# Linear attention: outputs ten chunks behind, and the image maps' small products moved behind transposes and grams

## The reference, cut to what matters

```python
qkv = x @ w_qkv.T                      # x: layer norm of h, (4, 3136, 192)
q, k, v = (qkv[0], qkv[1], qkv[2])     # 12 heads of 16 features
q = _l1_normalize(q)                   # divided by the sum over all tokens of |q|
k = _l1_normalize(k)
kv = jnp.einsum('bhnd,bhne->bhde', k, v)
out = jnp.einsum('bhnd,bhde->bhne', q, kv)
return out.transpose(0, 2, 1, 3).reshape(B, N, C) @ w_proj.T + b_proj
```

## Time and profile before

| | |
|---|---|
| median of 3 runs | 2784.31 us (2782.99 to 2789.03) |
| profiled execution | 2790.76 us, span 2788.9 us |
| mean granted TensorE clock | 0.894 |
| TensorE busy, whole span | 2293.3 us (82%) |
| VectorE busy | 2000.3 us (72%) |
| ScalarE busy | 1550.6 us (56%) |
| GpSimd busy | 996.8 us (36%) |
| the attention stage, 1883.00 to 2335.75 us | 452.75 us, TensorE clock 0.81 |

### The profile page before, as it was taken

One profiled execution on the slowest core, in us unless ns is written; L12 is line 12 of the kernel. 1 busy time (PEld: TensorE's weight loads), 2 busy tenths in 40 slices (PEclk: granted clock), 3 DMA queues, 4 the chain that ended last, 5 costly groups with the idle time before them and its releaser, 6 DMA issues. The chain is left out here.

```text
span 2788.9 us, 45419 instructions
## 1 busy us (share of the span) xinstructions
PE 2293.3 (82%) x14046; PEld 1665.0 (60%) x14047; DVE 2000.3 (72%) x5437; ACT 1550.6 (56%) x2693; POOL 996.8 (36%) x1024
## 2 busy tenths in 40 slices
PE   8999999999996888989865999926678885666665
PEld 4444444444444878888854999925576774444443
DVE  5777777777764888888853444447788877889986
ACT  2444444444444777777743566536665650777776
POOL 1100100100000355555561444468776730444443
PEclk9999999999997999999976999966787887677867
DMA  2000000000002011111125777731111100000000
GB/s 56 0 18 12 0 18 13 0 9 1 0 1 89 21 47 47 47 50 46 51 79 190 256 256 256 256 101 50 47 48 42 49 13 22 21 21 26 26 25 26
DMA packets 69143, 162.81 MB, mean 58 GB/s; under 512 B 12977, under 2 KB 32342, under 8 KB 68702
## 3 DMA queue, kind: packets, MB, share of 16 engines
q1 hardware_dynamic: 39426, 94.27, 10.3%
q0 software_dynamic: 21504, 44.99, 5.6%
q10 hardware_dynamic: 8064, 21.68, 2.6%
HBM read 63.98 MB, written 63.88 MB: 46 GB/s over the span
## 5 line engine op out<-in xcount | busy, mean ns | idle before, releaser
L211 ACT ACTIVATE prob<-pscore 128x896 f32<-128x896 f32 x336 | 308.1, 917 | 424.1 <-PE pscore L293 424.1
L418 DVE TENSOR_REDUCE pmax<-ppre 112x1 f32<-112x512 f32 x656 | 424.4, 686 | 162.7 <-PE ppre L260 162.6
L307 PE MATMUL pout<-prob,xkey 128*64 128x448 f32 x1344 | 328.3, 567 | 0.4 <-ACT prob L211 0.4
L260 PE MATMUL ppre<-xh,yh 49*112 49x512 f32 x656 | 291.5, 446 | 7.8 <-DVE pmax L418 4.1
L723 POOL DMA_INDIRECT rows_in<-xr,idx x224 | 231.4, 1033 | 154.4 <-DVE idx L1237 97.3
L1694 POOL DMA_INDIRECT yg<-rows_out,place x224 | 234.2, 1045 | 62.4 <-issue 62.1
L193 POOL CAST yh<-ynext 113x448 fp32r<-113x448 f32 x28 | 17.2, 616 | 668.1 <-DVE pmax L418 639.9
L260 PEld LDWEIGHTS ppre<-xh,yh 49*112 49x112 f32 x656 | 112.8, 172 | 239.8 <-issue 103.5
L293 PE MATMUL pscore<-yh,xh 49*128 49x448 f32 x700 | 241.3, 422 | 0.4 <-DVE yh L438 0.4
L2209 POOL TENSOR_TENSOR yg<-y,gout 112x512 f32<-112x512 f32 x112 | 141.3, 1273 | 259.1 <-DVE y L2442 259.1
L1544 POOL TENSOR_TENSOR zl<-z,zh 128x448 fp32r<-128x448 f32 x126 | 144.8, 1149 | 219.8 <-ACT zh L1510 210.3
(11 more groups left out here) (388 smaller groups left out, 6558.2 us busy)
## 6 DMA issues: line engine op xcount, KB each, us to landing
wd<-down SPq DMA_DIRECT2D x63, 512.0 KB, 3.0
xb<-rows_in SPq DMA_DIRECT2D x63, 448.0 KB, 3.6
rows_out<-yb ACTq DMA_DIRECT2D x63, 336.0 KB, 3.2
out<-ho SPq DMA_DIRECT2D x28, 336.0 KB, 2.8
rows_in<-zero SPq DMA_DIRECT2D x15, 448.0 KB
rows_in<-xr,idx POOLq DMA_INDIRECT x224
yg<-rows_out,place POOLq DMA_INDIRECT x224
xkey<-in_xkey SPq DMA_DIRECT2D x4, 800.0 KB, 6.7
```

The source lines that it names most:

```text
L211: nc.scalar.activation(prob[j % 3][:, :, :], pscore[j % 2][:, :, 0:CH], ACT.Exp).then_inc(exped, 1)
L260: pe.matmul(out[:, :], yh1[rows, q * T:(q + 1) * T], xh[b % 2][rows, block * 512:(block + 1) * 512], start=True, stop=True, tile_position= ...
L307: mm = pe.matmul(pout[i * LO:(i + 1) * LO, 0:CH], xkey[b % 2][:, 2 * j + i, :], prob[j % 3][:, i, :], start=(j == 0), stop=(i == 1 and j = ...
L418: nc.vector.reduce_max(pmax[:, q, 2 * block + half:2 * block + half + 1], bank(u, depth), AX.X).then_inc(pre_max, 1)
```

## The change

The lag of the outputs goes from nine chunks to ten and the ring from ten to eleven. On TensorE a step always begins with transposes and gram; the small products come behind them, and where there are outputs, the keys map, the projection and the image map come behind these. On VectorE `low` always opens a step; `values_mapped` moves behind `add_experts` of its step, `keys_mapped` and `map_projected` behind `add_moe`, and `image_mapped` behind `add_out`. Behind the loop one more chunk of outputs is left, and stands between values map and projection.

```diff
-    LATE = CPI + 2
+    LATE = CPI + 3
     RING = LATE + 1
...
             for s in range(NC):
                 b, c = divmod(s, CPI)
+                transposes(s)
+                gram(s, b, c)
+                if b and c == 0:
+                    turn_gram(b - 1)
                 if b and c == 1:
                     values_map(b - 1)
+                if s >= LATE:
+                    map_out(s - LATE)
                 if b and c == 2:
                     image_map(b - 1)
-                transposes(s)
-                if b and c == 0:
-                    turn_gram(b - 1)
-                gram(s, b, c)
                 if b and c == 0:
                     keys_map(b - 1)
                 if b and c == 1:
                     project_map(b - 1)
-                if s >= LATE:
-                    map_out(s - LATE)
...
             map_out(NC - LATE + 1)
             values_map(B - 1)
+            map_out(NC - LATE + 2)
             project_map(B - 1)
             image_map(B - 1)
-            for n in range(NC - LATE + 2, NC):
+            for n in range(NC - LATE + 3, NC):
                 map_out(n)
...
-                if s >= CPI and c == 1:
-                    values_mapped(b - 1)
-                if s >= CPI and c == 2:
-                    image_mapped(b - 1)
                 if s >= 0:
                     low(s)
...
                 if here(s + 3):
                     add_experts(s + 3)
+                if s >= CPI and c == 1:
+                    values_mapped(b - 1)
+                if here(s + 2):
+                    add_moe(s + 2)
                 if s >= CPI and c == 0:
                     keys_mapped(b - 1)
                 if s >= CPI and c == 1:
                     map_projected(b - 1)
-                if here(s + 2):
-                    add_moe(s + 2)
                 if s >= LATE:
                     add_out(s - LATE)
+                if s >= CPI and c == 2:
+                    image_mapped(b - 1)
...
             add_out(NC - LATE + 1)
             values_mapped(B - 1)
+            add_out(NC - LATE + 2)
             map_projected(B - 1)
             image_mapped(B - 1)
```

## The result

The change is slower: 2797.57 us (median of 7 runs, 2794.75 to 2805.5) against 2788.22 (7 runs, 2782.99 to 2789.87), a ratio of 1.0043 (95% interval 1.0027 to 1.0058). That is outside the predicted range of 2779 to 2795. Of the 9.5 us between the forecast of 2788.1 and the result, 3.9 are the base: the forecast stood on 2784.31, the median of 3 runs of the kernel before, where 7 runs give 2788.22. The profiled execution took 2794.75 us, span 2792.9.

What follows compares the result with a forecast made beforehand. GpSimd ends ordinary steps (13.85 us); boundary steps are longer because TensorE and VectorE hand small matrices through pqk_1. Boundaries +1.6 and +2.2 behind the loop gave +3.8 on 2784.31: 2788.1 us, range 2779 to 2795.

Steps and rivals of the forecast that it cites:

- The copies' place: At image boundaries, VectorE's later copies out of pqk_1 set the steps' lengths: 18.5, 16.8, 19.0 us; boundaries together +1.6 us.
- Predicted triples: Sums of the three steps building an image's map; second boundary 18.5 + 16.8 + 19.0 us, first boundary 2.1 less.
- predicted waits on TensorE: TensorE's waits for VectorE's copies in an image's first, second and third step: about 5.6, 3.0 and 4 to 5.6 us.
- the fourth step: The step after an image's three map steps: GpSimd has caught up, so it takes VectorE's own 12.87 us.
- The turn: In an image's first step, TensorE goes from gram into the turning transpose with under 1 us of waiting; before, 2.73 us.
- a low and a high case: An image's second step at TensorE's low clock, 17.9 us, or high clock, 15.5 us; the forecast took 16.8.
- The extra chunk: Behind the loop, one more chunk of outputs between values map and projection starts the projection 2.2 us later.
- The step that failed: Steps after the third boundary stay as they were, and everything behind the delayed projection stays the same: no added time.
- Low clock in all three steps: Rival: TensorE stays at the low clock in all boundary steps; triples 56.1 us, +9.2 in all, 2793.5; chance 0.31.
- The gap is really closed: Rival: q_and_k does not wait for the moved copies, boundary steps take GpSimd's 13.85 us; 2754 us; chance 0.01.

Runs made afterwards that it cites:

- image_early: The changed kernel with only the image copy moved earlier on VectorE, just behind `add_experts`; ratio 0.9967 to the kernel before.
- keys_early: The changed kernel with only the keys copy moved earlier on VectorE, ahead of the norm's sum; ratio 0.9965 to the kernel before.
- before_again: The kernel before, unchanged, measured and profiled a second time; ratio 1.0007 to the kernel before.
- all_early: The changed kernel with the image, keys and projection copies all moved just behind `add_experts`, TensorE's order kept; ratio 0.992 to the kernel before.
- gram_first: The kernel before with one move alone, the gram put ahead of the turning transpose; ratio 0.9989 to the kernel before.
- kept_warm: The changed kernel with 24, 11 and 22 spare matmuls ahead of the waiting second q-k product in an image's three steps; ratio 0.9957 to the kernel before.

## Why the prediction was wrong, and where it was right

**The copies' place** was right. Predicted triples were 52.2, 54.3 and 54.3, measured 51.9, 54.1 and 54.4; predicted waits on TensorE 5.6, 3.0 and 4 to 5.6, measured 6.1, 2.8 and 6.0; the fourth step was 12.87 as predicted. The turn waited 0.3 us. The boundaries cost +1.2 instead of +1.6. Which work would be slow behind the waits was right only in part. Timeline of TensorE in the change, steps 14 and 15:

```profile
2104.88 0.71 PE L1772 MATMUL pqk<-xh,wh 128*128 128x448 f32 x1 [6.10 <-DVE t L2045]
...
2108.48 0.93 PE L1739 MATMUL ptr<-eye,xn 112*128 112x112 f32 x8
...
2121.72 0.64 PE L1772 MATMUL pqk<-xh,wh 128*128 128x448 f32 x1 [2.76 <-DVE m L2057]
```

The products start at the low level behind 6.10, 2.76 and 6.03 us alike, and in the first two of these steps the level is back by the transposes (0.93 us). The forecast allowed for this return in the first and third step. For the second it took the middle of a low and a high case, and 16.8 against 16.91 owes something to luck: the products were low and the transposes high. The Trainium skill ("TensorE: Matmul & The Clock Gate", Part 1) has the throttled state as the one into which TensorE falls when it is idle; by that the trace agrees, with low products behind all three waits and transposes of 1.70 us behind the one of 6.03. Yet the triples did not go to the 56.1 of the rival that rests on that rule.

**The extra chunk** was right in its first part: where nothing slowed down (image_early, keys_early) the time from the start of step 27 to the image copy is 23.35 against 21.06 before, +2.3 for the predicted +2.2.

**The step that failed** is a pair of sentences: "The third boundary is followed by steps in which the gathers are over, and I leave those as they are", and behind the loop "everything behind is the same". Both terms were put at nothing, and together they measured about +6: the same instructions took longer. Steps 24 to 26 cost +2.9. Timeline of TensorE there:

```profile
2265.27 2.32 PE L1750 MATMUL pg<-xn 112*128 112x192 f32 x16
...
2276.07 0.74 PE L1772 MATMUL pqk<-xh,wh 128*128 128x448 f32 x1 [3.79 <-ACT junk L1916]
...
2278.11 1.70 PE L1739 MATMUL ptr<-eye,xn 112*128 112x112 f32 x8
```

and of the kernel before, the same places:

```profile
2267.40 1.50 PE L1739 MATMUL ptr<-eye,xn 112*128 112x112 f32 x8
2268.70 3.44 PE L1750 MATMUL pg<-xn 112*128 112x192 f32 x16
...
2278.98 0.47 PE L1772 MATMUL pqk<-xh,wh 128*128 128x448 f32 x1 [2.13 <-ACT junk L1915]
```

In the change TensorE did transposes and gram at the high level (2.32 us for the gram, where the kernel before took 3.44). It was done early and stood 3.79 us waiting for ScalarE's sum, where the kernel before waited 2.13. The wait ended at the same place, 20.56 and 20.58 us into the stretch; the loss lies behind it, where the change did products and transposes at the low level. The kernel before shows something else that the prediction's reading of the earlier trace rows passed over: behind the wait of 2.01 us the products are at the high level, but the transposes and the gram after them are slower than in the change. Behind the loop the cost was +5.4 instead of +2.2: the image map took 2.77 instead of 2.05, and the last eight chunks 25.33 instead of 23.00. I had priced the clock only where the change moved something; it also differed in places that the change does not touch. What of this the shift in time decides, and what else does, stays open.

Sum in the traces, with -0.3 in steps 0 to 6: -0.3 + 1.2 + 2.9 + 5.35 = 9.1, the 451.59 - 442.46 measured there, and close to the 9.35 between the medians. Of it 3.5 are what I had predicted in kind and size (+1.2, +2.3), and some 6 (2.9 + 5.35 - 2.3) are the clock behind the last boundary. On the base of 2788.22 the forecast of +3.8 would have been 2792.0; the 5.5 us that are left lie in these two places. Steps 24 to 26 and the end carry the loss in the second profiles too, but less of it: over both profiles of each kernel the stage takes 442.5 and 443.9 us before and 451.6 and 451.4 in the change, of which the boundaries are +1.8, steps 24 to 26 +2.1 and the end +4.5. The 6 us are then 4.3. A warning against reading this too finely: the two profiled spans differ by 4.0 only, because everything outside the stage, which the change does not touch, took 5.1 us less in the changed one; and before_again, with 33.84 and 45.81, has 3.3 of those 6 us in the kernel before too.

**"Low clock in all three steps"** was the rival with 0.31, and its +9.2 is nearly the measured +9.35 (its time, 2793.5, has the base 3.9 too low), for a cause in the wrong place: the triples did not grow to 56.1. **"The gap is really closed"** was refused rightly: it needed the copies early, and even all_early makes a triple of 45, not 41.6.

**What I missed for readers of the diff:** TensorE's new order need not cost anything. all_early has it unchanged, with the copies early, and is 0.8% faster than the kernel before. What the boundaries lose lies in VectorE's list. That the new order is a gain by itself is not shown, since no run has it with VectorE's old list.

**Open** is what starts the low level behind the loop, where kernels with the same instructions and waits differ, and why TensorE, once low there, stays low through many outputs in the change. For steps 24 to 26 the runs give more: the length goes with TensorE's wait for ScalarE's sum 20.6 us into the stretch. Where it was 1.01 to 2.17 us (six profiles) the stretch took 32.2 us, at 2.20 to 2.34 (three) it took 33.8 to 33.9, and at 3.79 to 3.81 (five) 35.1 to 35.2. The five are the ones with step 25's transposes at the high level (0.93 us). Lag ten with the old order was not tried: the image map would be overwritten before the older image's last outputs have read it.

## What to carry to other kernels

When several products share one PSUM buffer, the copy that empties it belongs as early in the copying engine's list as its data allow, and ahead of bulk work that nobody waits for: three such copies moved ahead of 4.4 to 6.5 us of sums were worth 1.2% here (1.0043 against 0.992), what the clock gave back included, in the boundaries and behind them. When an engine's list is shortened, look which wait stands behind it, as in gram_first. And price every stretch behind a change at both of TensorE's levels when it follows a wait of 1 to 4 us; a few filler matmuls in such a wait are a cheap test, and can be a gain. Before an effect is put down to a wait, look for a kernel that has the same wait without it. And take the base of a forecast from more than three runs.

## What the runs showed of the hardware that I had not expected

Spare matmuls shortened the kernel: eight at the end took the ratio from 1.0044 to 1.0004, and the kernel with 171 at the boundaries stands at 0.9957, with a part of that from the end. The length of the one wait ahead does not decide the level alone, as my prediction assumed: behind the loop, waits of 1.09 and 0.70 us were followed by the low level in the change and, with the same instructions, by the high level in keys_early. After 2.01 us has products at the high level, and after 2.76 us the change has them at the low one.

A matmul that starts a sum in one part of a bank disturbed a sum left open in another: in kept_warm the spare products with the start flag wrote columns 64 to 511, the open gram lay in columns 0 to 63, and the output moved by 0.073 in relative error. The Trainium skill says so ("PSUM — Partial Sum Buffer", "The four PSUM rules"): the start flag clears the written marks of the whole bank on the partitions it touches, so that the next adding matmul overwrites. The run agrees with it; that the gram alone is what changed was not measured apart.
